# A graph transformer layer on one core: the edge stage's two one-hot matrices, one moved from VectorE to ScalarE, one cut in four

## The chip, the core and the metric

One core of one Trainium2 chip runs the whole program. The metric is the device time of one launch in microseconds (us); lower is better. The engines are TensorE (PE, with its weight loads as PEld), VectorE (DVE), ScalarE (ACT), GpSimd (POOL) and SyncE (SP). Each takes its own instructions in order, and they wait for each other on semaphores.

## What is computed

The reference is a graph neural network of two layers over 6,250 nodes with 128 features and 200,000 edges sorted by destination, with 32 edge types and 16 node types, and 8 heads of 16 features:

```python
def gt_layer(x, ntype, etype, src, dst, ...):
    k = typed_linear(x, ntype, Wk).reshape(n, H, HS)      # q and v alike
    kT = jnp.einsum('nhd,htdo->nhto', k, Watt)            # vT = ... v, Wmsg
    kw = kT[src, :, etype]
    m = vT[src, :, etype]
    a = jnp.einsum('ehd,ehd->eh', kw, q[dst]) * pri[:, etype].T / SQRT_D
    att = edge_softmax(a, dst, n)
    msg = (m * att[:, :, None]).reshape(-1, H * HS)
    hag = jax.ops.segment_sum(msg, dst, num_segments=n)
    h = jax.nn.silu(typed_linear(hag, ntype, Wa))
    alpha = jax.nn.sigmoid(skip[ntype])[:, None]
    h = h * alpha + x * (1.0 - alpha)
    # then mean and variance over the features, scale and shift
```

After two such layers there is a last product, the sum with the input, and a normalisation.

## The kernel before

A first part sorts out the edges (ranks, starts of segments, types). Then a loop over the two layers runs these stages, one after the other: the projections q, k, v; a table with one row for each pair of source node and edge type (`table_d`, 256 numbers to a row, k then v); **the edge stage**; a stage that joins sums across tiles of edges; and the output projection with its normalisation.

The edge stage takes the edges in chunks of 16 tiles (CT) of 128 edges. There are 98 chunks for each of the two layers, 196 in all. Nearly everything in it is double buffered (index b, 0 or 1), and the loop body stands twice, once for each b. A quarter of a chunk is 4 tiles (QT). The order is written out by hand:

- **POOL** issues one indirect DMA for each tile (L903), 16 to a chunk, that gathers the rows of 128 edges out of `table_d` into `kv_e`. It waits for the indices of the chunk (`row_s`, copied by ACT in L999) and, at each quarter, for the values `pv` of the chunk two before (L901), which read the same buffer.
- **SP** loads `local_b` (L915: for each edge of the chunk its rank relative to the tile's first, in bf16, the same 2048 numbers on all 128 partitions) and `q_w` (the q rows of the ranks). It does so two chunks ahead, after the products `qe_ps` of the chunk that used that buffer (L914).
- **PE** multiplies `of_rank` with `q_w` (L1033, one quarter at a time) to spread q from ranks to edges. It does this for chunk c+1 while it is in chunk c: quarters 0 to 2 at the start of its body, and quarter 3 after the transpose of `score` (L1053) and the two products of flags (L1056). Then come the transpose of `prob_t` (L1060) and the sums `sum_ps` (L1067), which multiply `to_rank` with `pv`, 3 tiles to a bank. A product of two f32 tiles is two instructions in the trace.
- **DVE** forms `kq` (L966) and `score` (L969) by quarters as the gathers land, two running maxima (L975, L977), `below` (L980) and the four products `pv` (L985).
- **ACT** copies indices (L999), `score_t` (L1001), takes the exponential (L1003), copies the probabilities into `pv` (L1010), the sums out of PSUM (L1019), and issues the store of the chunk (L1023).

Two matrices of ones and zeros are needed for each chunk, both f32, 128 partitions by 16 tiles by 128. `of_rank` has ranks on the partitions and edges along the row: `local_b` equals the partition's number `part`. DVE makes it in `spread_ranks` (L944), one instruction, for chunk c+2, between `below` and `pv` of chunk c. `to_rank` has edges on the partitions and ranks along the row: `lane` (0 to 127) equals `local_c` of the edge. DVE makes it in `place_edges` (L949), one instruction, for chunk c+1, after quarter 2 of chunk c; it waits for the sums that last read that buffer (`s_used`).

## Time and profile before

| | us |
|---|---|
| median of 3 runs | 8303.22 |
| the runs | 8294.33 to 8305.0 |
| profiled execution: from its first to its last instruction (span) | 7619.3 |
| median less that span | 683.9 |
| edge stage: start of the first to start of the last gather, layer 0 | 1329.92 to 3534.96 |
| the same, layer 1 | 4809.19 to 7010.65 |

The profile gives the execution's time as its span; the program's time on the device holds in addition what lies ahead of the first instruction and behind the last. An engine's busy share is its mean over stages that have different limits, so the edge stage has to be read by itself. In the views each row has the engine, the line of the code, the operation, the tile written and the tiles read, and in brackets the idle time of the engine before the row and what ended it. "Issue" is time in which the engine waited for nothing that the profile shows.

### The profile page before, as it was taken

To read this page: it belongs to the slowest core of one execution; us is meant where nothing else is said; L and a number is where in the kernel's file an instruction comes from. 1 tells how busy PE (TensorE), PEld (TensorE's weight loads), DVE (VectorE), ACT (ScalarE), POOL (GpSimd) and SP (SyncE) were. 2 spreads that over 40 slices of the span, in tenths; PEclk is the share of its full clock that TensorE was granted. 3 is DMA by queue.
4 is the path that set the end of the run, shared out by engine and by line. 5 is a ranking of instruction groups with operands and counts; after the bars stand their busy time and mean duration, and the time that the engine had idled before them with its cause. 6 is when DMAs were issued, how large, how long until landed. Compare 5 with 4: busy or idle time off the path is not lost. (4 is left out here: it accounts for less than half of the span.)

```text
span 7619.3 us, 79126 instructions
## 1 busy us (share of the span) xinstructions
PE 4483.6 (59%) x18423; PEld 3236.2 (42%) x18424; DVE 3763.8 (49%) x5261; ACT 1445.3 (19%) x3714; POOL 4322.7 (57%) x4007
## 2 busy tenths in 40 slices
PE   0128999566666665654318999566666665665221
PEld 0113443555555555554203444455555555555111
DVE  1224443555555555554374444455555555554473
ACT  0013333111111111112112333111111111111111
POOL 0543222777777777775303222677777777776305
PEclk9569999666766666666559999766666666676555
DMA  3125776666666666665103777666666666666101
GB/s 68 39 45 220 297 297 281 160 178 166 177 165 176 167 171 170 170 172 122 29 19 150 297 297 296 181 168 174 169 173 168 176 166 176 169 173 159 34 0 35
DMA packets 809561, 1228.51 MB, mean 161 GB/s; under 512 B 152983, under 2 KB 623978, under 8 KB 758833
## 3 DMA queue, kind: packets, MB, share of 16 engines
q0 software_dynamic: 223248, 853.51, 33.6%
q10 hardware_dynamic: 439680, 221.74, 11.4%
q1 hardware_dynamic: 146097, 148.81, 10.9%
q14 instruction: 528, 4.33, 0.2%
q8 instruction: 8, 0.13, 0.0%
HBM read 574.03 MB, written 649.66 MB: 161 GB/s over the span
## 5 line engine op out<-in xcount | busy, mean ns | idle before, releaser
L903 POOL DMA_INDIRECT kv_e<-table_d,row_s x3136 | 3453.7, 1101 | 982.1 <-issue 939.1
L1033 PE MATMUL qe_ps<-q_w,of_rank 128*128 (+1 forms) x6336 | 1149.3, 340 | 634.5 <-DVE kq L966 565.9
L1067 PE MATMUL sum_ps<-pv,to_rank 128*128 128x136 f32 x6272 | 1193.2, 373 | 261.7 <-DVE pv L985 261.7
L1033 PEld LDWEIGHTS qe_ps<-q_w,of_rank 128*128 128x128 f32 x6336 | 991.3, 240 | 767.4 <-issue 710.9
L966 DVE TENSOR_TENSOR kq<-kv_e,qe_ps 128x512 f32<-128x512 f32 x784 | 537.4, 685 | 1528.8 <-DMA kv_e<-table_d,row_s 1526.7
L1067 PEld LDWEIGHTS sum_ps<-pv,to_rank 128*128 128x128 f32 x6272 | 1154.7, 277 | 318.4 <-issue 318.4
L759 POOL DMA_INDIRECT table_d<-piece,t_row x392 | 372.7, 951 | 1041.9 <-ACT piece L811 829.7
L811 DVE COPY piece<-k_ps 128x512 f32<-128x512 f32 x784 | 541.7, 691 | 808.6 <-PE k_ps L801 808.6
L801 PE MATMUL k_ps<-edge_w,kv_t 128*128 128x512 f32 x1568 | 813.9, 601 | 2.6 <-DVE edge_w L821 2.6
L801 PE MATMUL v_ps<-edge_w,kv_t 128*128 128x512 f32 x1568 | 802.4, 593 | 0.0
L1019 ACT COPY sums<-sum_ps 128x408 f32<-128x408 f32 (+1 forms) x1176 | 522.5, 461 | 943.9 <-PE sum_ps L1067 941.8
L811 ACT COPY piece<-v_ps 128x512 f32<-128x512 f32 x784 | 458.7, 585 | 898.4 <-PE v_ps L801 898.4
L1053 PE MATMUL turn_ps_<-ident,score 128*128 128x128 f32 x196 | 93.0, 475 | 866.9 <-DVE score L969 866.9
L969 DVE TENSOR_REDUCE score<-kq 128x32 f32<-128x512 f32 x784 | 537.8, 686 | 26.9
L985 DVE TENSOR_TENSOR pv<-kv_e,pv 128x512 f32<-128x512 f32 x784 | 491.6, 690 | 24.3 <-ACT pv L1010 0.4
L801 PEld LDWEIGHTS v_ps<-edge_w,kv_t 128*128 128x128 f32 x1568 | 298.4, 190 | 377.0 <-issue 330.2
L951 DVE TENSOR_TENSOR to_rank<-lane,local_c 128x2048 f32<-128x2048 f32 x198 | 452.1, 2283 | 0.0
L801 PEld LDWEIGHTS k_ps<-edge_w,kv_t 128*128 128x128 f32 x1568 | 283.0, 190 | 357.9 <-issue 284.4
L1053 PEld LDWEIGHTS turn_ps_<-ident,score 128*128 128x128 f32 x196 | 35.7, 182 | 912.7 <-DVE score L969 912.7
L999 ACT COPY row_s<-row_c 128x16 int32 x196 | 40.0, 204 | 1751.3 <-DMA kv_e<-table_d,row_s 1751.3
L715 POOL DMA_INDIRECT q_d<-qkv,qrow_i x98 | 95.1, 971 | 407.6 <-DVE qkv L618 407.6
L975 DVE TENSOR_TENSOR_SCAN run_max<-turn_ps_,score_t 128x128 f32<-128x128 f32 x196 | 83.1, 424 | 394.8 <-ACT score_t L1001 394.8
(269 smaller groups left out, 3352.6 us busy)
## 6 DMA issues: line engine op xcount, KB each, us to landing
part_d<-sums ACTq DMA_DIRECT2D x196, 1088.0 KB, 6.4
local_b<-local_d SPq DMA_DIRECT2D x200, 512.0 KB, 6.4
kv_e<-table_d,row_s POOLq DMA_INDIRECT x3136, 2.8
q_w<-q_d SPq DMA_DIRECT2D x200, 64.0 KB
table_d<-piece,t_row POOLq DMA_INDIRECT x392, 4.5
flag<-start_d SPq DMA_DIRECT2D x392, 8.0 KB
q_d<-zero SPq DMA_DIRECT2D x50, 64.0 KB
max_d<-ends_max ACTq DMA_DIRECT2D x196, 1.0 KB, 4.3
```

The lines of the kernel that those rows point to most:

```text
L759: pool.indirect_dma_start(out=piece_rows, out_offset=bass.IndirectOffsetOnAxis(ap=row_s[:, j, q:q + 1], axis=0), in_=piece[:, q].rearrange ...
L801: pe.matmul(bank[:, g % 2, :], kv_t[:, slot[j], a, :], edge_w[:, a, g * TG:(g + 1) * TG, :].rearrange("p t o -> p (t o)"), start=True, sto ...
L811: copy(piece[:, q, o:o + TG, a * D:(a + 1) * D], bank[:, g % 2, :].rearrange("p (t o) -> p t o", t=TG)).then_inc(s_copied, 1)
L903: pool.indirect_dma_start(out=kv_e[:, b, t, :], out_offset=None, in_=table_d, in_offset=bass.IndirectOffsetOnAxis(ap=row_s[:, b, t:t + 1], ...
L951: dve.tensor_tensor(to_rank[:, b], lane[:].unsqueeze(1).broadcast_to([P, CT, P]), local_c[:, ds(c * CT, CT)].unsqueeze(2).broadcast_to([P, ...
L966: dve.tensor_tensor(kq[:, ts], kv_e[:, b, ts, 0:D], qe_ps[:, q * QT * D:(q + 1) * QT * D].rearrange("p (t f) -> p t f", t=QT), ALU.mult).t ...
L969: dve.tensor_reduce(score[:, q * QT * H:(q + 1) * QT * H], kq[:, ts].rearrange("p t (h d) -> p (t h) d", h=H), AX, ALU.add).then_inc(s_sco ...
L985: dve.tensor_tensor(pv[:, b, ts, 0:D].rearrange("p t (h d) -> p t h d", h=H), kv_e[:, b, ts, D:2 * D].rearrange("p t (h d) -> p t h d", h= ...
L1019: last = act.copy(sums[:, b, t0:t1, :], sum_ps[:, n % 3, 0:(t1 - t0) * REC].rearrange("p (t f) -> p t f", f=REC)).then_inc(s_sumc[n % 3], 1)
L1033: last = pe.matmul(qe_ps[:, t * D:(t + 1) * D], of_rank[:, b, t, :], rows, start=True, stop=True)
L1053: pe.transpose(turn_ps[:, 0, :], score[:], ident[:])
L1067: last = pe.matmul(sum_ps[:, n % 3, (t - t0) * REC:(t - t0 + 1) * REC], to_rank[:, b, t, :], pv[:, b, t, :], start=True, stop=True)
```

## The change

`of_rank` is made by ACT, in two passes over 128x2048: the absolute value of (`local_b` minus the partition's number), with a new one-column tile `minus` as bias, and then, in place, the positive part of (1 minus that). The result is 1 where they are equal and 0 elsewhere. The second pass waits for the first on a new semaphore. In the loop both stand at the end of ACT's body, after the store of the chunk; ahead of the loop ACT makes the first two. `to_rank` stays on DVE, in four instructions of 128x512, two after quarter 1 and two after quarter 2.

```diff
-            def spread_ranks(dve, c, b, i):
-                dve.wait_ge(s_loc[b], (i + 1) * 16)
-                dve.tensor_scalar(of_rank[:, b].rearrange("p t e -> p (t e)"), local_b[:, b, :], part[:], None,
-                                  ALU.is_equal).then_inc(s_of[b], 1)
-
-            def place_edges(dve, c, b, i):
+            def spread_ranks(act, b, i):
+                act.wait_ge(s_loc[b], (i + 1) * 16)
+                act.activation(of_rank[:, b].rearrange("p t e -> p (t e)"), local_b[:, b, :], ACT.Abs, bias=minus[:]).then_inc(s_far[b], 1)
+                act.wait_ge(s_far[b], i + 1)
+                act.activation(of_rank[:, b].rearrange("p t e -> p (t e)"), of_rank[:, b].rearrange("p t e -> p (t e)"), ACT.Relu, bias=1.0, scale=-1.0).then_inc(s_of[b], 1)
+
+            def place_edges(dve, c, b, i, q):
                 dve.wait_ge(s_used[b], ONE + i)
-                dve.tensor_tensor(to_rank[:, b], lane[:].unsqueeze(1).broadcast_to([P, CT, P]),
-                                  local_c[:, ds(c * CT, CT)].unsqueeze(2).broadcast_to([P, CT, P]), ALU.is_equal).then_inc(s_to[b], 1)
+                dve.tensor_tensor(to_rank[:, b, q * QT:(q + 1) * QT], lane[:].unsqueeze(1).broadcast_to([P, QT, P]),
+                                  local_c[:, ds(c * CT + q * QT, QT)].unsqueeze(2).broadcast_to([P, QT, P]), ALU.is_equal
+                                  ).then_inc(s_to[b], 1)
...
-                            if q == 2:
-                                place_edges(dve, c + 1, 1 - b, i + b)
+                            if q in (1, 2):
+                                place_edges(dve, c + 1, 1 - b, i + b, 2 * q - 2)
+                                place_edges(dve, c + 1, 1 - b, i + b, 2 * q - 1)
...
-                        spread_ranks(dve, c + 2, b, i + 1)
                         dve.wait_ge(s_pcol[b], i + 1)
...
                         act.dma_start(out_d[ds(c, 1), :, :, :].rearrange("a j t f -> j (a t) f"), sums[:, b]).then_inc(s_out[b], 16)
+                        spread_ranks(act, b, i + 1)
...
-                        pe.wait_ge(s_to[b], i + 1)
+                        pe.wait_ge(s_to[b], (i + 1) * 4)
```

On DVE, in the second half of the loop body (b = 1), from quarter 2 to the products `pv`, the rows of the kernel before are:

```order
L966 TENSOR_TENSOR kq<-kv_e,qe_ps 128x512
L969 TENSOR_REDUCE score<-kq 128x32
L951 ISA
L951 TENSOR_TENSOR to_rank<-lane,local_c 128x2048
L966 TENSOR_TENSOR kq<-kv_e,qe_ps 128x512
L969 TENSOR_REDUCE score<-kq 128x32
L975 SCALAR_TENSOR_TENSOR run_max<-turn_ps_,score_t 128x128
L977 SCALAR_TENSOR_TENSOR rank_max<-turn_ps_,run_max 128x128
L980 TENSOR_TENSOR below<-score_t,rank_max 128x128
L946 TENSOR_SCALAR of_rank<-local_b,part 128x2048
L985 TENSOR_TENSOR pv<-kv_e,pv 128x4x128 x4
```

The same place in the changed kernel, from the end of quarter 1 to quarter 3's product:

```order
L972 TENSOR_REDUCE score<-kq 128x32
L952 REGISTER_ALU
L953 ISA
L953 TENSOR_TENSOR to_rank<-lane,local_c 128x512
L953 ISA
L953 TENSOR_TENSOR to_rank<-lane,local_c 128x512
L969 TENSOR_TENSOR kq<-kv_e,qe_ps 128x512
L972 TENSOR_REDUCE score<-kq 128x32
L953 ISA
L953 TENSOR_TENSOR to_rank<-lane,local_c 128x512
L953 ISA
L953 TENSOR_TENSOR to_rank<-lane,local_c 128x512
```

The long instruction behind quarter 2 has become two pairs of short ones, behind quarters 1 and 2, and nothing stands any more between `below` and `pv`.

On ACT, from the last copies of a chunk's sums (b = 0) to the next chunk's start, the kernel before has, with the semaphores that each row waits for:

```order
L1019 COPY sums<-sum_ps 128x136 [waits e_used0]
L1022 REGISTER_ALU
L1023 ISA [waits e_sumc2,e_sumc1,e_sumc0]
L1023 DMA part_d<-sums 128x16x136
L999 ISA [waits e_kv12,e_kv13,e_kv11,e_kv10]
L999 COPY row_s<-row_c 128x16
```

and the changed kernel:

```order
L1025 COPY sums<-sum_ps 128x136 [waits e_used0]
L1028 REGISTER_ALU
L1029 ISA [waits e_sumc2,e_sumc1,e_sumc0]
L1029 DMA part_d<-sums 128x16x136
L946 REGISTER_ALU
L947 ACTIVATE of_rank<-local_b,minus 128x2048 [waits e_loc0]
L949 ACTIVATE of_rank<-of_rank 128x2048 [waits e_far0]
L1005 ISA [waits e_kv12,e_kv13,e_kv11,e_kv10]
L1005 COPY row_s<-row_c 128x16
```

Two long instructions have come in behind the store and ahead of the wait for the next chunk's gathers.

## Rows read from the trace of the kernel before

**Rows 1.** The page: span, busy us, and busy tenths in 40 slices.
```profile
span 7619.3 us, 79126 instructions
PE 4483.6 (59%) x18423; PEld 3236.2 (42%) x18424; DVE 3763.8 (49%) x5261; ACT 1445.3 (19%) x3714; POOL 4322.7 (57%) x4007
...
POOL 0543222777777777775303222677777777776305
PEclk9569999666766666666559999766666666676555
```

**Rows 2.** Groups of instructions: count, busy us, mean ns of one, idle before.
```profile
L903 POOL DMA_INDIRECT kv_e<-table_d,row_s x3136 | 3453.7, 1101 | 982.1 <-issue 939.1 <-DVE pv L985 43.0
...
L985 DVE TENSOR_TENSOR pv<-kv_e,pv 128x512 f32<-128x512 f32 x784 | 491.6, 690 | 24.3 <-ACT pv L1010 0.4
...
L951 DVE TENSOR_TENSOR to_rank<-lane,local_c 128x2048 f32<-128x2048 f32 x198 | 452.1, 2283 | 0.0
...
L946 DVE TENSOR_SCALAR of_rank<-local_b,part 128x2048 f32<-128x2048 bf16 x200 | 257.5, 1287 | 38.3 <-DMA local_b<-local_d 38.3
```

**Rows 3.** The tile kv_e: shortest, median and longest gather, first and last start.
```profile
L903 POOL DMA_INDIRECT kv_e<-table_d,row_s x3136: 942/946/3054, 1329.9 to 7010.7; - x196
```

**Rows 4.** Timeline at one to_rank: start, us, engine, line [idle before].
```profile
2406.80 2.28 DVE L951 TENSOR_TENSOR to_rank<-lane,local_c 128x2048 f32<-128x2048 f32 x1
2407.49 2.40 POOL L903 DMA_INDIRECT kv_e<-table_d,row_s  x1 [0.30 <-issue]
```

**Rows 5.** Timeline, the same chunk, from the transpose of score to the store.
```profile
2413.31 0.47 PE L1053 MATMUL turn_ps_<-ident,score 128*128 128x128 f32 x1 [5.84 <-DVE score L969]
...
2414.86 2.08 PE L1033 MATMUL qe_ps<-q_w,of_rank 128*128 x8
...
2416.39 1.32 DVE L946 TENSOR_SCALAR of_rank<-local_b,part 128x2048 f32<-128x2048 bf16 x1
2416.45 1.38 POOL L903 DMA_INDIRECT kv_e<-table_d,row_s  x1 [0.30 <-issue]
...
2417.79 2.54 DVE L985 TENSOR_TENSOR pv<-kv_e,pv 128x512 f32<-128x512 f32 x4
2418.13 1.17 POOL L903 DMA_INDIRECT kv_e<-table_d,row_s  x1 [0.31 <-issue]
...
2418.73 5.69 PE L1067 MATMUL sum_ps<-pv,to_rank 128*128 128x136 f32 x32 [1.38 <-DVE pv L985]
2419.61 0.95 POOL L903 DMA_INDIRECT kv_e<-table_d,row_s  x1 [0.30 <-issue]
...
2420.48 0.50 ACT L1019 COPY sums<-sum_ps 128x408 f32<-128x408 f32 x1 [2.73 <-PE sum_ps L1067]
...
2421.84 0.50 ACT L1019 COPY sums<-sum_ps 128x408 f32<-128x408 f32 x1 [0.86 <-PE sum_ps L1067]
...
2425.13 0.39 ACTq L1023 DMA_DIRECT2D part_d<-sums  x1
```

**Rows 6.** Timeline, 22 us earlier: quarters 0 to 2 of the next chunk's product.
```profile
2403.26 2.02 PE L1033 MATMUL qe_ps<-q_w,of_rank 128*128 128x128 f32 x16
...
2406.31 1.15 PE L1033 MATMUL qe_ps<-q_w,of_rank 128*128 x8 [1.03 <-DVE kq L966]
```

**Rows 7.** The chunk after: its gather in to_rank, and its wait for indices.
```profile
2430.99 2.28 DVE L951 TENSOR_TENSOR to_rank<-lane,local_c 128x2048 f32<-128x2048 f32 x1
2432.09 1.99 POOL L903 DMA_INDIRECT kv_e<-table_d,row_s  x1 [0.30 <-issue]
...
2434.05 0.20 ACT L999 COPY row_s<-row_c 128x16 int32 x1 [9.15 <-DMA kv_e<-table_d,row_s]
```

**Rows 8.** Groups of ACT's instructions, SBUF to SBUF, in other stages.
```profile
L628 ACT ACTIVATE hag<-h_sb 128x3200 f32<-128x3200 f32 x2 | 5.7, 2872 | 150.8 <-DVE h_sb L647 150.8
...
L1138 ACT ACTIVATE tile_lm<-tile_lm 128x1568 f32<-128x1568 f32 x2 | 3.0, 1510 | 10.8 <-DVE tile_lm L1161 10.8
```

**Rows 9.** DMA issues: KB each, median us to landing.
```profile
part_d<-sums ACTq DMA_DIRECT2D x196, 1088.0 KB, 6.4
```

More of the change, by code:

```diff
@@ L857, in program @@
         to_rank = sb(st, "to_rank", [P, 2, CT, P])
+        minus = sb(st, "minus", [P, 1])
         kq = sb(st, "kq", [P, CT, D])
@@ L875, in program @@
             (s_idx, s_q, s_loc, s_flag, s_of, s_to, s_qe, s_kq, s_score, s_turn, s_turned, s_scan, s_below, s_exp,
-             s_prob, s_pcol, s_used, s_ends, s_endsd, s_out, s_go) = (two(n) for n in (
+             s_prob, s_pcol, s_used, s_ends, s_endsd, s_out, s_go, s_far) = (two(n) for n in (
                  "idx", "q", "loc", "flag", "of", "to", "qe", "kq", "score", "turn", "turned", "scan", "below",
-                 "exp", "prob", "pcol", "used", "ends", "endsd", "out", "go"))
-            s_win = sem("e_win")
+                 "exp", "prob", "pcol", "used", "ends", "endsd", "out", "go", "far"))
+            s_win, s_minus = sem("e_win"), sem("e_minus")
             s_kv = [[sem(f"e_kv{b}{q}") for q in range(4)] for b in range(2)]
@@ L942, in _ @@
                     sp.wait_ge(s_q[b], (NCH // 2 + 1) * 16)
-            def spread_ranks(dve, c, b, i):
-                dve.wait_ge(s_loc[b], (i + 1) * 16)
-                dve.tensor_scalar(of_rank[:, b].rearrange("p t e -> p (t e)"), local_b[:, b, :], part[:], None,
-                                  ALU.is_equal).then_inc(s_of[b], 1)
-            def place_edges(dve, c, b, i):
+            def spread_ranks(act, b, i):
[4 more added lines that the diff above has]
+            def place_edges(dve, c, b, i, q):
                 dve.wait_ge(s_used[b], ONE + i)
-                dve.tensor_tensor(to_rank[:, b], lane[:].unsqueeze(1).broadcast_to([P, CT, P]),
-                                  local_c[:, ds(c * CT, CT)].unsqueeze(2).broadcast_to([P, CT, P]), ALU.is_equal).then_inc(s_to[b], 1)
+                dve.tensor_tensor(to_rank[:, b, q * QT:(q + 1) * QT], lane[:].unsqueeze(1).broadcast_to([P, QT, P]),
+                                  local_c[:, ds(c * CT + q * QT, QT)].unsqueeze(2).broadcast_to([P, QT, P]), ALU.is_equal
+                                  ).then_inc(s_to[b], 1)
             @block.vector
             def _(dve):
-                for b in range(2):
-                    spread_ranks(dve, b, b, 0)
-                place_edges(dve, 0, 0, 0)
+                dve.tensor_scalar(minus[:], part[:], -1.0, None, ALU.mult).then_inc(s_minus, 1)
+                for q in range(4):
+                    place_edges(dve, 0, 0, 0, q)
                 with dve.Fori(0, NCH // 2) as i:
@@ L993, in _ @@
                     act.copy(row_s[:, b, :], row_c[:, b * CT:(b + 1) * CT]).then_inc(s_idx[b], 1)
+                act.wait_ge(s_minus, 1)
+                for b in range(2):
+                    spread_ranks(act, b, 0)
                 with act.Fori(0, NCH // 2) as i:
```

## The prediction

> **What bounds the kernel now.** I read the stage's length first. The two stretches of gathers last 2205 and 2201 us of the span of 7619.3, and nothing outside them is edited, so only they count. The page's means do not tell what limits them (POOL 57%, PE 59%, DVE 49%) [rows 1]. The group of gathers does: 3136 of them, 1101 ns each, with 982.1 us of idle time between them, 0.31 each, nearly all "issue" [rows 2]. A chunk is 16 x (1.101 + 0.313) = 22.6 us with the two entries into the stage, 22.5 by the stretches (4406.5 / 196 = 22.48). POOL thus never waits for data inside the stage; in the timeline every gather starts 0.30 or 0.31 us after the last one ended. **POOL's issue of gathers sets the time**, and a microsecond taken from it in each chunk is worth 196 us.
>
> Next I look at what makes a gather long. The median is 946 ns, the longest 3054 [rows 3], the mean 1101 [rows 2]: 3136 x 0.155 = 486 us lie above the median, 2.5 us a chunk. The timeline shows where. A gather that starts 0.69 us into the instruction that writes `to_rank` takes 2.40 us and ends 0.80 us after it, as if only its first 0.15 us had been done before [rows 4]; the one a chunk later takes 1.99 and also ends 0.81 after [rows 7]. A gather that starts with `of_rank` takes 1.38, and the next, which starts 0.34 us into the four `pv` products, 1.17; the one after that starts 1.82 us into them, and takes the undisturbed 0.95 [rows 5]. Sorted in this way, the timeline's 3136 gathers (first and last in [rows 3]) give: 196 held by `to_rank`, 295 us together, **1.5 us a chunk**; 198 held by `of_rank`, 157 us, **0.8 a chunk**; the rest 38 us, mostly `pv`, **0.2 a chunk**. Without stalls a chunk would be 16 x (0.946 + 0.305) = **20.0 us**.
>
> The Trainium skill ("SBUF — State Buffer", section Who interferes with whom) has the rule for this: a VectorE instruction with two SBUF inputs contends with a GpSimd instruction that reads SBUF, one in a two-port mode with any, and the shared port is held for the whole instruction. The trace agrees for both kinds [rows 4, 5].
>
> **The change, part by part.**
>
> *`of_rank` leaves DVE.* That takes 1.29 us of DVE work from between `below` and `pv` of each chunk [rows 2], and the stall with it: the sorting above leaves nothing of the 486 us for ACT, which copies 0.50 us at a time beside the gathers [rows 5]. Gain 0.8 us a chunk. `pv` itself waits for the copy of probabilities and does not start earlier, so nothing on PE's side gains.
>
> *`to_rank` in four.* A DVE instruction of 128x512 with such operands takes 0.69 (`pv`, [rows 2]), so four are 2.76 in place of 2.28. DVE then has 0.8 us a chunk less work than before in all, and is idle about half of the time [rows 1]: it costs nothing. What counts is how long a gather is held. It is caught at one point early in its life, and then for the rest of the short instruction. Bounds for a chunk: zero, if no gather's start falls into the pieces; above, each pair lasts 1.4 us, about one gather period, so it catches one or two gathers for at most 0.45 us each, 1.8 for both pairs. The nearest row is `pv`, four such pieces back to back, which cost the gather 0.22 and the following one nothing [rows 5]: so the port is let go between the pieces. I take 0.2 for each pair, 0.4 together, instead of 1.5. `pv` was partly shielded, since `of_rank` had just set POOL's phase; I raise it from 0.2 to 0.3, bounds 0.2 and 0.6. Sum of stalls: 0.4 + 0.3 = **0.7 us a chunk** (from 0.3 to 2.2) in place of 2.5.
>
> *ACT's two passes.* ACT takes 1510 ns for 128x1568 and 2872 for 128x3200 [rows 8], 0.835 ns an element, so 1.91 us for 2048; two with a semaphore between them, 3.9 us. Reading bf16 is not in the trace; I take the same. ACT stands idle for 9.15 us ahead of the next index copy [rows 7], so the copy of indices is not late. No table load comes with them in ACT's order. Here is a rule that speaks against the change: the Trainium skill ("ScalarE: Activation LUTs", section Rules for kernel authors) wants relu on VectorE, where it is up to three times faster. The trace agrees on the price (1.29 against 3.9 us), but by [rows 2] DVE's instruction also stops POOL. The same page (What ACT_TABLE_LOAD costs) gives about 1990 ns for such a pass with a bias by pointer, which would add 0.2 us to the ring below.
>
> *The new wait.* PE's quarters 0 to 2 for the next chunk need the new `of_rank`, which ACT now makes behind the store. Before, they followed the sums at once. Now: the sums end at 2424.42, the store is issued at 2425.13 and takes 0.39 [rows 5], then 3.9 us: PE starts about **5.1 us after the sums**. Behind its wait stand quarters 0 to 2, then L1053 and all of the chunk's chain. The cover is PE's idle time before L1053, 5.84 us [rows 5]. This closes a ring: L1053 to the end of the sums 11.1 us [rows 5] + 5.1 + quarters 0 to 2. These were 2.02 + 1.15 = 3.2 us [rows 6] at the high clock; at the low one a quarter is 2.08 [rows 5], so 6.2. The ring is 19.4 to 22.4 us. As long as it is under POOL's 20.7, nothing shows; above, it becomes the period. The granted clock in the stage reads 0.6 to 0.7 [rows 1], between the levels 0.5 (1.2 GHz) and 1 (2.4 GHz). In the row of sums the first two copies are 1.36 us apart; at that pace 16 tiles would take 7.25, and they took 5.69 [rows 5]: the clock rose under way, after 3 to 4 us of dense work. If quarters 0 to 2 do the same, they take 3.7 + 0.41 x 3.2 = 5.0, and the sums, now behind denser work, about 1 us less (wholly at the high clock 3.7). That is 11.1 + 5.1 + 5.0 - 1.0 = **20.2 us**: under POOL's period, by little.
>
> *Ends of the stage.* The first `of_rank` is 2.6 us later, but the first `kq` waits for gathers anyway; the last two passes lie under the landing of the store, 6.4 us [rows 9]. Both zero.
>
> **Sum.** 20.0 + 0.7 = 20.7 us a chunk against 22.5: 1.8 x 196 = 353 us. The span goes from 7619.3 to about 7266; with the 683.9 outside it, as in the median of the runs, the time from 8303 to **7950**.
>
> **The rivals.**
>
> 1. *The ring sets the period (PE waits for ACT, ACT for PE).* For it: 20.2 is an estimate between 19.4 and 22.4, and POOL can wait for `pv` of two chunks before (L901). Against it: when PE is late it has no idle time before L1053, and dense work raised the clock in the row of sums. With the ring at 21.0 to 22.3 the time is 8010 to 8265, centre 8090.
> 2. *Short pieces still stall POOL.* If the port is not let go between two pieces, each pair holds a gather for up to 1.2, with `pv` 2.2 in all: period 22.2, time 8245; if half of that, 8100. Against: the 0.95 gather within `pv` [rows 5].
> 3. *Slower.* The gap of 5 us leaves PE at the low clock throughout: quarters 6.2, sums 7.25. The ring is then 11.1 + 1.6 + 5.1 + 6.2 = 24.0, 1.5 over the old period: 8303 + 290 = 8600. It decides from a ring of 22.5, that is when sums and quarters together lose more than 1.3 us against [rows 5] and my 5.0 us. Against: the sums would have to be slower than before though more work stands ahead of them.
> 4. *Nothing changes*, since ring or another wait comes out at 22.4 to 22.6: for it only the ring's upper bound.
>
> **How the numbers follow.** Forecast 0.60 (7870 to 8040), rival 1 0.24, rival 2 0.08, slower 0.05, no change 0.03. The range of 8 in 10 is 7870 to 8160: it holds the forecast's own bounds of stalls (0.3 to 1.1 us) and the lower half of rivals 1 and 2. A difference of 0.2% (17 us) is about what a measurement of this kernel can tell from no change. Faster by more than that: 0.60 + 0.24 + 0.08 = 0.92, less 0.01 for the top of rival 1: 0.91. Same 0.04, slower 0.05.
>
> **What would show it.** Right: the mean of a gather falls from 1101 to about 990 ns; its idle time stays at 0.31 and "issue"; no gather over about 1.6 us in the stage; DVE's `to_rank` about 690 ns each; ACT's passes about 1.9 us; PE's idle time before L1060 (the old L1053) a few tenths, put down to `score`. Rival 1: gathers as short, but POOL waits for `pv`, and PE's row before the transpose of `score` has no idle time. Rival 2: gathers of 1.5 to 2 us beside the pairs. Rival 3: PE's clock at 0.5 all through the stage. The forecast is wrong if ACT's pass over bf16 takes well over 2 us, or if the time of a chunk is over 21.2.

## The result: 3.9% slower in the comparison, 5.0% faster on another chip

| kernel | us, median | range |
|---|---|---|
| before | 8298.77 | 8278.49 to 8305.0 |
| changed | 8613.93 | 8610.93 to 8617.45 |

The changed kernel takes 1.0386 of the time before, with a 95% interval of 1.0346 to 1.0425. The prediction was 7950 and faster; it was wrong.

One fact has to stand ahead of all numbers. The experiments below fell on six chips, and these show two kinds. On chips 13 and 6 the kernel before takes 7627 to 7631 us (medians of the jobs), on chips 10, 9, 4 and 7 it takes 8278 to 8319, and no execution of it lay between 7638 and 8227. Only chip 10 was met in two jobs, so whether it is the chip or something else of the job that makes the kind is not shown. So every time below stands beside the kernel before of its own job. The kernel before, on record at 8303 us, and its profile with a span of 7619.3 [rows 1] are one of each kind. I call the kinds **prompt** (7630) and **late** (8300), for the reason shown below; the texts of expectation say "first chip" and "second chip".

The page of the changed kernel's profiled execution, of the late kind (span, busy us, and busy tenths in 40 slices, as in [rows 1]):

```profile
span 8609.1 us, 80616 instructions
PE 4410.2 (51%) x18423; PEld 3276.0 (38%) x18424; DVE 3533.9 (41%) x5657; ACT 2219.3 (26%) x4114; POOL 3955.2 (46%) x4007
...
POOL 0632224555555555554203223555555555555304
PEclk9579997777677767776559998776766666766655
```

This execution took 8610.93 us, 1.8 more than its span. So only some 2 us lie outside the span, not the 683.9 that the prediction put there.

Groups of instructions of the same execution (busy us, mean ns | idle before and what ended it), beside [rows 2]:

```profile
L904 POOL DMA_INDIRECT kv_e<-table_d,row_s x3136 | 3085.6, 984 | 2272.8 <-DVE pv L988 1329.3 <-issue 929.5 <-ACT row_s L1005 14.0
...
L953 DVE TENSOR_TENSOR to_rank<-lane,local_c 128x512 f32<-128x512 f32 x792 | 511.9, 688 | 452.9 <-PE sum_ps L1074 319.8 <-remote 71.2 <-issue 61.9
...
L988 DVE TENSOR_TENSOR pv<-kv_e,pv 128x512 f32<-128x512 f32 x784 | 489.5, 687 | 261.0 <-ACT pv L1016 261.0
```

A gather has become short, as forecast: 984 ns instead of 1101. But POOL, whose gaps in [rows 2] are 0.31 us each, now waits for `pv` 1329.3 us. The longest waits of DVE, ACT and POOL (us in total, times, longest us):

```profile
DVE run_max L979 <- ACT score_t L1007: 2351.0, 196, 13.8
ACT score_t L1007 <- remote: 2305.8, 192, 13.6
POOL kv_e L904 <- DVE pv L988: 1329.3, 192, 10.3
```

"Remote" is not an engine. ACT's copy of `score_t` waits for nothing but the semaphore of the transposes on PE; the word says that when it was released no instruction had just ended. The timeline of one chunk shows it (start, us, engine, line [idle before]):

```profile
2419.29 0.27 PE L1060 MATMUL turn_ps_<-ident,score 128*128 128x128 f32 x1
2419.50 0.71 PE L1063 MATMUL turn_ps_<-flag,spread 16*128 16x128 f32 x4
...
2423.64 0.95 POOL L904 DMA_INDIRECT kv_e<-table_d,row_s  x1 [0.30 <-issue]
2427.27 0.27 ACT L1007 COPY score_t<-turn_ps_ 128x128 f32<-128x128 f32 x1 [12.33 <-remote]
...
2430.11 2.50 DVE L988 TENSOR_TENSOR pv<-kv_e,pv 128x512 f32<-128x512 f32 x4 [1.34 <-ACT pv L1016]
2430.94 6.03 PE L1074 MATMUL sum_ps<-pv,to_rank 128*128 128x136 f32 x32 [1.29 <-DVE pv L988]
2431.59 1.24 POOL L904 DMA_INDIRECT kv_e<-table_d,row_s  x1 [7.01 <-DVE pv L988]
...
2443.47 5.46 PE L1040 MATMUL qe_ps<-q_w,of_rank 128*128 128x128 f32 x24 [6.50 <-ACT of_rank L949]
...
2448.72 0.33 PE L1060 MATMUL turn_ps_<-ident,score 128*128 128x128 f32 x1
```

PE is done with the flags at 2420.21, and ACT starts at 2427.27, 7.06 us later. In between POOL issues its last gathers; the last begins at 2423.64, and then POOL is stuck behind `pv`. The trace also records when each semaphore rises. The one of the flags' products rises at 2427.25, in one burst with three others of PE, of which the oldest had been due since 2418.56. The ends of PE's instructions are modelled in the trace, so one has to ask whether the products themselves came late. The burst speaks against it: by their rows the four products end over 2.7 us (2418.56 to 2421.29), and their semaphores rise within 0.25. Over all chunks the lateness has a median of 5.65 us (4.7 to 7.5 in nine of ten), and it is found only where PE raises the semaphore. Where ACT or DVE raise it, the next engine starts at once: `run_max` 0.03 us after the copy of `score_t`, and the exponential 0.03 after `below`, in all 196 chunks.

In every one of the 192 late chunks ACT's copy starts 2.2 to 3.0 us after the end of the last gather, and in nine of ten 0.8 to 1.5 after the end of the last packet of POOL's DMA queue. So in this kernel the semaphores come when the stream of gathers has run out; the trace does not tell whether POOL's issuing or the traffic of its gathers counts.

### The profile page after: what moved, and what is told of

It is laid out like the page before. It is cut to its first block and busy times, and to the rows that moved or that the text cites. A ratio compares the mean times of both kernels' runs of the same rounds, so it can differ in the third digit from the quotient of the medians.

```text
span 8609.1 us, 80616 instructions
## 1 busy us (share of the span) xinstructions
PE 4410.2 (51%) x18423; PEld 3276.0 (38%) x18424; DVE 3533.9 (41%) x5657; ACT 2219.3 (26%) x4114; POOL 3955.2 (46%) x4007
## 5 line engine op out<-in xcount | busy, mean ns | idle before, releaser
L904 POOL DMA_INDIRECT kv_e<-table_d,row_s x3136 | 3085.6, 984 | 2272.8 <-DVE pv L988 1329.3
L1040 PE MATMUL qe_ps<-q_w,of_rank 128*128 (+1 forms) x6336 | 1256.8, 380 | 1206.1 <-ACT of_rank L949 1128.9
L1040 PEld LDWEIGHTS qe_ps<-q_w,of_rank 128*128 128x128 f32 x6336 | 1172.7, 286 | 1268.0 <-issue 702.0
L1074 PE MATMUL sum_ps<-pv,to_rank 128*128 128x136 f32 x6272 | 1135.0, 360 | 263.3 <-DVE pv L988 263.3
L1074 PEld LDWEIGHTS sum_ps<-pv,to_rank 128*128 128x128 f32 x6272 | 1096.5, 265 | 319.8 <-issue 319.8
L1067 PE MATMUL turn_ps_<-ident,prob_t 128*128 128x128 f32 x196 | 92.9, 474 | 1287.6 <-ACT prob_t L1009 1287.6
L953 DVE TENSOR_TENSOR to_rank<-lane,local_c 128x512 f32<-128x512 f32 x792 | 511.9, 688 | 452.9 <-PE sum_ps L1074 319.8
L1007 ACT COPY score_t<-turn_ps_ 128x128 f32<-128x128 f32 x196 | 52.2, 266 | 2364.2 <-remote 2305.8
L1067 PEld LDWEIGHTS turn_ps_<-ident,prob_t 128*128 128x128 f32 x196 | 35.6, 182 | 1324.9 <-ACT prob_t L1009 1324.9
L947 ACT ACTIVATE of_rank<-local_b,minus 128x2048 f32<-128x2048 bf16 x200 | 400.4, 2002 | 145.5 <-ACT sums L1025 84.3
```

The costliest lines, as they stand in the source:

```text
L904: pool.indirect_dma_start(out=kv_e[:, b, t, :], out_offset=None, in_=table_d, in_offset=bass.IndirectOffsetOnAxis(ap=row_s[:, b, t:t + 1], ...
L947: act.activation(of_rank[:, b].rearrange("p t e -> p (t e)"), local_b[:, b, :], ACT.Abs, bias=minus[:]).then_inc(s_far[b], 1)
L953: dve.tensor_tensor(to_rank[:, b, q * QT:(q + 1) * QT], lane[:].unsqueeze(1).broadcast_to([P, QT, P]), local_c[:, ds(c * CT + q * QT, QT)] ...
L1040: last = pe.matmul(qe_ps[:, t * D:(t + 1) * D], of_rank[:, b, t, :], rows, start=True, stop=True)
L1074: last = pe.matmul(sum_ps[:, n % 3, (t - t0) * REC:(t - t0 + 1) * REC], to_rank[:, b, t, :], pv[:, b, t, :], start=True, stop=True)
```

## Experiments

Letters stand for theories. A is the ring through ACT (PE waits for `of_rank`, rivals 1 and 3 of the prediction). B is that the pairs of short instructions hold up POOL. D came up after the first late runs: an unbroken stream of gathers on POOL holds back PE's semaphores.

The diffs show the lines that matter; new tiles, new semaphores and their start values are left out.

### The kernel before, and each half of the change by itself (chip 13, prompt)

e1 is the kernel before once more. e2 has only `to_rank` in four:

```diff
-                            if q == 2:
-                                place_edges(dve, c + 1, 1 - b, i + b)
+                            if q in (1, 2):
+                                place_edges(dve, c + 1, 1 - b, i + b, 2 * q - 2)
+                                place_edges(dve, c + 1, 1 - b, i + b, 2 * q - 1)
```

e3 has only `of_rank` on ACT:

```diff
-                        spread_ranks(dve, c + 2, b, i + 1)
...
+                        spread_ranks(act, b, i + 1)
```

e4 is e2 with two passes of the same size and form added to ACT at that place, on tiles that nobody reads, while DVE still makes `of_rank`:

```diff
+                        act.activation(idle_rank[:], lane_w[:], ACT.Abs, bias=part[:]).then_inc(s_idle, 1)
+                        act.wait_ge(s_idle, c * 2 + 1)
+                        act.activation(idle_rank[:], idle_rank[:], ACT.Relu, bias=1.0, scale=-1.0).then_inc(s_idle, 1)
+                        act.wait_ge(s_idle, c * 2 + 2)
```

> The kernel before, profiled a second time. Its profile had a span of 7619 us beside runs of 8299, and the changed kernel's span is 8609 beside 8614. If 684 us lie outside the span of this program, the span is again about 7619 and the time about 8300. If the first profile caught an execution that differs from the timed ones, the span is now about 8297, and the gathers have idle time that ends on pv, or the copy of score_t waits several us more than the 2.8 us of the first profile.

> Only the cut of to_rank into four, of_rank stays on DVE. Theory A (the new wait of PE for ACT makes the ring the period): no ring is closed here, so the time is under the kernel before. If POOL's issue sets the time of the timed runs too, a chunk loses 1.1 us of stalls: 8300 - 215 = about 8085. Theory B (the pairs of short instructions on DVE are what is late): slower than before, towards 8600. Theory C (the timed runs of before are not set by POOL's stalls): within 0.5% of before.

> Only the move of of_rank to ACT, to_rank stays one instruction on DVE. Theory A: the whole loss is here, 8550 to 8650, a chunk at about 27 us, and POOL waits for pv of two chunks before. Theory B: about the time of before or under it.

> of_rank stays on DVE and to_rank is cut in four; ACT makes two passes of 128x2048 at the same place behind the store, but over a constant into a tile that nobody reads, so that PE does not wait for them (extra work, nothing left out). Theory A (it is PE's wait): the same time as with the cut alone. Rival (ACT is too busy, its other copies come late): about 8600.

| run | us | ratio to before (7631.13) | 95% |
|---|---|---|---|
| e1 before | 7631.45 | 1.0001 | 0.9991 to 1.0011 |
| e2 split only | 7376.36 | 0.9668 | 0.9652 to 0.9684 |
| e3 ACT only | 7473.41 | 0.9798 | 0.9781 to 0.9814 |
| e4 split, ACT busy beside it | 7375.62 | 0.9668 | 0.9652 to 0.9684 |

This was the surprise that opened the case: the kernel that had been timed at 8299 ran at 7631, and the pieces of a change that had cost 3.9% were both gains. Groups of e2:

```profile
L903 POOL DMA_INDIRECT kv_e<-table_d,row_s x3136 | 3216.5, 1026 | 982.1 <-issue 959.9 <-DVE pv L988 22.3
```

and of e3:

```profile
L904 POOL DMA_INDIRECT kv_e<-table_d,row_s x3136 | 3311.5, 1056 | 982.2 <-issue 962.4 <-DVE pv L985 19.8
...
L947 ACT ACTIVATE of_rank<-local_b,minus 128x2048 f32<-128x2048 bf16 x200 | 400.3, 2002 | 146.0 <-ACT sums L1022 139.1 <-DMA local_b<-local_d 6.9
L949 ACT ACTIVATE of_rank<-of_rank 128x2048 f32<-128x2048 f32 x200 | 381.9, 1910 | 6.3
```

In both, POOL's idle time is the 982 us of [rows 2], 0.31 for each gather, and only the gathers' busy time falls. The split gives 254.8 us, 1.30 a chunk; ACT gives 157.7, 0.80 a chunk. e4 shows that two passes of ACT, when nobody waits for them, cost nothing beside the gathers (0.7 us of 7376). A and B have no room here: POOL has no wait beyond its usual gaps, and what the pairs still hold up is within the mean of 1026.

### The same on a late chip (chip 10)

> The changed kernel a second time. In the last experiments the kernel before took 7631 us, as in its first profile, and not 8299 as in the comparison of the change; there each half of the change alone gained 2 and 3.3%. If the changed kernel's loss belongs to the executions in which the kernel before takes 8299, it now takes the forecast's share: both halves together remove the stalls, 20.7 us a chunk, 7631 - 353 = about 7280, with score_t copied about 2 us after its transpose. If the ring of PE and ACT is slow by itself when both halves are there, it is again about 8610, with a copy of score_t 12 us after PE's first quarter.

> The cut of to_rank alone, beside the changed kernel in the same job. If the kernel before is again at 7631: about 7376, and above the changed kernel by about 100. If the kernel before is at 8299 in this job: this shows whether the slower executions take the gain of the cut away (then within 1% of 8299).

> The kernel before, profiled in the same job as the two kernels below, so that all three are read on one chip. The jobs so far fell on two chips: on one the kernel before takes 7631 us and TensorE's semaphores are raised 0.01 us after its products end; on the other it takes 8308, and in the changed kernel the products of quarters 1 to 3 and the flags end 6 to 10 us before their semaphores rise. If this job is on the second chip: a period of about 25.9 us a chunk, with such late semaphores too, but fewer. If it is on the first: 7631.

> The changed kernel. On the first chip: POOL's gathers set the period, stalls of 0.6 to 0.7 us a chunk, 20.7 us a chunk, about 7280 (the theory that the late semaphores make the whole loss); a ring of PE and ACT above that gives 7340 to 7600. On the second chip: again 8615.

| run | us | before in the job | ratio | 95% |
|---|---|---|---|---|
| e5 changed kernel | 8618.23 | 8307.55 | 1.0380 | 1.0353 to 1.0408 |
| e6 split only | 8579.48 | 8307.55 | 1.0335 | 1.0299 to 1.0370 |
| e7 before | 8316.39 | 8301.51 | 1.0015 | 0.9989 to 1.0041 |
| e8 changed kernel | 8619.03 | 8301.51 | 1.0402 | 1.0366 to 1.0439 |

The same text of e2 that gained 3.3% loses 3.3% here. The group of gathers in e6:

```profile
L903 POOL DMA_INDIRECT kv_e<-table_d,row_s x3136 | 3069.1, 979 | 2261.8 <-DVE pv L988 1316.1 <-issue 943.5 <-ACT row_s L1002 2.1
```

e6 has no work on ACT at all, so the loss is not the ring through ACT as I had drawn it. What it shares with the changed kernel is the wait for `pv`, and 2863.5 us in which ACT's copy of `score_t` is released by "remote". The kernel before has the same illness, in part of its chunks. Its gathers in e7:

```profile
L903 POOL DMA_INDIRECT kv_e<-table_d,row_s x3136 | 3349.3, 1068 | 1703.2 <-issue 973.0 <-DVE pv L985 730.1
```

and its timeline, one bad chunk (from 2417) and the start of the next:

```profile
2417.52 1.22 PE L1056 MATMUL turn_ps_<-flag,spread 16*128 16x128 f32 x4
...
2429.70 0.27 ACT L1001 COPY score_t<-turn_ps_ 128x128 f32<-128x128 f32 x1 [14.50 <-remote]
...
2434.02 1.24 POOL L903 DMA_INDIRECT kv_e<-table_d,row_s  x1 [7.46 <-DVE pv L985]
```

The flags end at 2418.74 and are seen at 2429.70, 11 us late. POOL waits for `pv` in 74 chunks of 196 here, and in 192 in the changed kernel. Not all of these late copies of `score_t` wait for the end of the stream: of the 64 that start over 1 us late, a quarter start within 0.25 us of a gather's end.

### Does breaking the stream release the semaphores? (chip 10)

e9 is the changed kernel with one unused fill on POOL ahead of gather 12 of each chunk:

```diff
+                            if t == 12:
+                                pool.memset(pause[:], 0.0).then_inc(s_pause, 1)
+                                pool.wait_ge(s_pause, i * 2 + b + 1)
```

> The changed kernel, with GpSimd writing zeros to an unused tile of 128x2048 before the last four gathers of each chunk, about 2 us in which it issues none (extra work, nothing left out). Theory D (on the second chip TensorE's semaphores rise only once the stream of gathers breaks off): they rise in the pause, the copy of score_t comes some 5 us earlier, and in spite of the pause the time is 200 to 900 us under the 8615 of the changed kernel. Rival (the delay is of a fixed length, or due to the density of TensorE's instructions): the time stays at 8615 or rises by up to 400. On the first chip the pause is only added: 196 x 2 = 400 us above the changed kernel.

8445.57 us (two runs, 8417.38 and 8473.76), 1.0193 of before (1.0127 to 1.0260), 173 less than e8 in the same job, a little under the 200 to 900 that I expected. Its groups:

```profile
L908 POOL DMA_INDIRECT kv_e<-table_d,row_s x3136 | 3059.8, 976 | 1758.4 <-issue 1011.9 <-DVE pv L992 693.9 <-POOL pause L902 52.0
...
L902 POOL MEMSET pause<- 128x2048 f32 x196 | 357.1, 1822 | 0.1
```

357 us of useless work were put on the engine that was thought to bound the kernel, and it became faster. POOL's wait for `pv` fell from 1326 (e8) to 694 us, in 95 chunks instead of 192. So the pattern of POOL's instructions, or of the traffic that its gathers start, has a part in when PE's semaphores are seen. No theory of the prediction has that.

### The changed kernel on a prompt chip (chip 6)

> The changed kernel, in a new job. On the chip where the kernel before takes 7631: 7260 to 7340, POOL's gathers back to back at 20.7 us a chunk, score_t copied within 3 us after its transpose starts. On the chip where it takes 8300: 8618 again.

> Only the move of of_rank to ACT; to_rank stays one instruction of 2.3 us that holds a gather for 1.5 us in each chunk. On the first chip 7473 again. On the second, theory D (an unbroken stream of gathers keeps TensorE's semaphores back, and each hold of the stream lets them through): under the cut alone (8579) and the changed kernel (8618), near the 8300 of the kernel before, since the long hold is still there. Rival (the ring over ACT makes the loss there): 8550 or more, as the changed kernel.

e12 paces the stream with a fill of 128x512 before each quarter:

```diff
+                            if t % QT == 0:
+                                pool.memset(pause[:], 0.0).then_inc(s_pause, 1)
+                                pool.wait_ge(s_pause, i * 8 + b * 4 + t // QT + 1)
```

> The changed kernel, with GpSimd writing zeros to an unused tile of 128x512 before each quarter's gathers, four pauses of about 0.6 us in a chunk where the pause of 1.8 us stood once (extra work, nothing left out). On the first chip POOL's period is longer by four such writes: 196 x 2.6 = 500 us over the changed kernel. On the second, theory D in the form that any break in the stream helps: as with the one pause, 8350 to 8500. If only a long break drains what is held back: 8600 or more.

| run | us | ratio to before (7627.31) | 95% |
|---|---|---|---|
| e10 changed kernel | 7246.10 | 0.9499 | 0.9472 to 0.9527 |
| e11 ACT only | 7470.11 | 0.9793 | 0.9764 to 0.9821 |
| e12 changed, paced | 8110.86 | 1.0633 | 1.0602 to 1.0664 |

Here the forecast stands: its span was about 7266, and the measured one is 7246.7 (for e10 I had expected 7260 to 7340). The page of e10:

```profile
span 7246.7 us, 80616 instructions
PE 4294.4 (59%) x18423; PEld 3176.4 (44%) x18424; DVE 3564.0 (49%) x5657; ACT 2229.5 (31%) x4114; POOL 3950.5 (55%) x4007
...
PEclk9559999777777777776558999877777777776555
```

its gathers, as a group:

```profile
L904 POOL DMA_INDIRECT kv_e<-table_d,row_s x3136 | 3082.2, 983 | 982.4 <-issue 961.7 <-DVE pv L988 20.7
```

as a tile (shortest, median, longest), against 942/946/3054 in [rows 3]:

```profile
L904 POOL DMA_INDIRECT kv_e<-table_d,row_s x3136: 942/946/1468, 1330.8 to 6639.0; - x196
```

and once round the ring in its timeline:

```profile
2406.21 0.27 PE L1060 MATMUL turn_ps_<-ident,score 128*128 128x128 f32 x1
2406.41 0.71 PE L1063 MATMUL turn_ps_<-flag,spread 16*128 16x128 f32 x4
...
2407.16 0.27 ACT L1007 COPY score_t<-turn_ps_ 128x128 f32<-128x128 f32 x1 [2.27 <-PE turn_ps_ L1063]
...
2410.95 5.63 PE L1074 MATMUL sum_ps<-pv,to_rank 128*128 128x136 f32 x32 [1.53 <-DVE pv L988]
...
2421.91 4.71 PE L1040 MATMUL qe_ps<-q_w,of_rank 128*128 128x128 f32 x24 [5.33 <-ACT of_rank L949]
...
2426.47 0.33 PE L1060 MATMUL turn_ps_<-ident,score 128*128 128x128 f32 x1
```

Gathers 983 ns, gaps 0.31, none over 1.47 us; the flags end at 2407.12 and are seen at 2407.16, as in all 196 chunks of every prompt run. The ring in this round, from one L1060 to the next, is 20.26 us, and POOL's chunk (3082.2 + 982.4) / 196 = 20.74. The two are nearly tied: PE's wait for `score` before L1060, 5.84 us in [rows 5], is down to 116.6 us in all, 0.6 a chunk.

e12 tells what time on POOL is worth when POOL does bound the kernel:

```profile
L908 POOL DMA_INDIRECT kv_e<-table_d,row_s x3136 | 3083.1, 983 | 1398.9 <-issue 762.2 <-POOL pause L902 636.7
...
L902 POOL MEMSET pause<- 128x512 f32 x784 | 425.0, 542 | 26.1 <-issue 25.8
```

The gathers are unchanged and POOL's busy and idle time grew by 425.0 + 26.1 + (1398.9 - 982.4) = 868 us; the time grew by 865. The 500 expected left out that after each fill POOL waits 0.81 us (636.7 / 784) instead of 0.30. Fills cost all their time here, and a fill gave time back on chip 10. The two kinds have different bounds.

### A wait instead of a fill, and half the data (chip 9, late)

e14 lets POOL go on to gather 12 only when the chunk before has had its `score` transposed. e15 gathers 128 numbers instead of 256 for each edge, out of other rows, and `pv` is made from what was gathered instead of from the v half, so its values are not the reference's.

```diff
+                            if t == 12:
+                                pool.wait_ge(s_turned[1 - b], ONE + i + b)
```

```diff
-                            pool.indirect_dma_start(out=kv_e[:, b, t, :], out_offset=None, in_=table_d,
+                            pool.indirect_dma_start(out=kv_e[:, b, t, 0:D], out_offset=None, in_=table_d.rearrange("r (a f) -> (r a) f", a=2),
```

> Only the move of of_rank to ACT, wanted on the second chip (the one where the kernel before takes 8300). Theory D (an unbroken stream of gathers keeps back TensorE's semaphores; the long to_rank instruction breaks it): 8250 to 8500, under the 8579 of the cut alone and the 8618 of both. Rival (on this chip the ring over ACT costs as much by itself): 8550 or more. On the first chip 7470 again, which tells nothing new.

> The changed kernel; POOL in addition waits, before the last four gathers of a chunk, until ACT has copied score_t of the chunk before. On the first chip that copy is made long before, by the fourth gather: no change, 7246. On the second, theory D: the stream breaks off after 12 gathers in place of 16, TensorE's semaphores rise some 2.5 us later, and the last four gathers are issued beside scans and pv, where POOL stood idle for 7 us: 3 us a chunk less, 7900 to 8300. Rival (the delay has nothing to do with the stream): later still than 8618, as POOL stands twice.

> The changed kernel with gathers of half the row, 128 numbers of 256 (the products pv take the same half twice; the values are left out and other rows are read). POOL issues as many gathers in the same time, but the DMA engines move half the bytes. On the first chip POOL's issue still sets the time: 7200 to 7250. On the second: if the bytes that the gathers move keep TensorE's semaphores back, the loss goes and the time is 7250 to 7500; if it is POOL's issue or the number of rows and semaphore writes, which stay, 8550 to 8620.

| run | us | ratio to before (8277.51) | 95% |
|---|---|---|---|
| e13 ACT only | 8610.05 | 1.0409 | 1.0340 to 1.0478 |
| e14 changed, waits at gather 12 | 8295.13 | 1.0027 | 0.9995 to 1.0059 |
| e15 changed, half the numbers | 8653.26 | 1.0462 | 1.0399 to 1.0524 |

e13 refutes a part of D: I had thought that the long `to_rank`, which holds a gather for up to 2 us, breaks the stream and so protects the kernel before. e13 has the long `to_rank` and is as slow as the changed kernel. Its semaphores are late in another way. The flags are over 1 us late in only 93 chunks (median over all 0.84), half of those are seen within 0.2 us of a gather's end, in the midst of the stream, and the copy of `prob_t`'s transpose into `pv` (L1013) comes late too: 1.40 us after the product in the median, against 0.29 in e10. Its gathers:

```profile
L904 POOL DMA_INDIRECT kv_e<-table_d,row_s x3136 | 3306.7, 1054 | 2027.1 <-DVE pv L985 1068.7 <-issue 957.5 <-ACT row_s L1002 0.9
```

e15 says that it is not the bytes: with half of them the wait for `pv` is no shorter, 1404.8 us. e14 is some 320 us under the changed kernel's 8614 to 8619 on other late chips, and its timeline shows why:

```profile
2414.88 0.71 PE L1065 MATMUL turn_ps_<-flag,spread 16*128 16x128 f32 x4
...
2415.62 0.27 ACT L1009 COPY score_t<-turn_ps_ 128x128 f32<-128x128 f32 x1 [6.42 <-PE turn_ps_ L1065]
...
2416.70 0.95 POOL L906 DMA_INDIRECT kv_e<-table_d,row_s  x1 [5.79 <-ACT score_t L1009]
```

While POOL stands still, the flags' semaphore is seen 0.03 us after the products (2415.59 to 2415.62). Over all chunks ACT starts 0.04 us after them in the median and 0.99 at most, in 155 of 196 within 0.05: the row put down to "remote" for 2305.8 us is gone. But lateness has moved to the other semaphores of PE: DVE's `to_rank` now waits 1206.8 us for "remote".

### The wait in the kernel before, and the last two runs (chips 4 and 7, late)

e16 puts the same wait into the kernel before; e17 and e18 are e14 again.

> The kernel before with one wait of POOL ahead of a chunk's gather 12, for the copy score_t of the chunk before; nothing else is changed. Two kinds of chip have been seen. On the kind where TensorE's semaphores rise late (before about 8300): if the unbroken stream of gathers holds them back, the wait breaks the stream at a set place, score_t is copied within 0.1 us of the flags' products, and the time goes below before's own by 100 us or more (about 8000 to 8200). If the lateness has nothing to do with the stream, the wait only takes time from POOL: 8300 to 8500. On the kind where they rise in time (before about 7630): POOL at gather 12 is 16 to 17 us into a chunk of 22.5 and the score of the chunk before is turned at about 6 to 8 us, so the wait is always met: 7631, within 0.3%.

> The changed kernel with the same wait, as run before in e14. On the kind of chip with late semaphores: 8295 again, equal to the kernel before. On the other kind: gather 12 of a chunk starts about 15.5 us after the chunk's first gather and score_t of the chunk before is there by 8 us at the latest, so the wait costs nothing and the time is that of the changed kernel there, 7246, within 0.3%. If it costs on that kind what the paced kernel lost (865), it comes out near 8100, and the waits of POOL themselves are what hurts there.

> The same kernel as e14 and e17: the changed kernel with POOL's wait for score_t ahead of gather 12. Seen twice, both times beside a kernel before of about 8300: 8295 and 8312. If before runs at about 7630 here, the wait should always be met (gather 12 starts about 15.5 us after a chunk's first gather, score_t is there by 8 us) and the time is 7246, within 0.3%; about 8100, the loss of the paced kernel, if waits of POOL themselves cost on that kind of chip. If before runs at about 8300 here, 8300 again.

| run | chip | us | before in the job | ratio | 95% |
|---|---|---|---|---|---|
| e16 before, waits at gather 12 | 4 | 8189.75 | 8291.93 | 0.9897 | 0.9826 to 0.9968 |
| e17 changed, the same | 4 | 8311.79 | 8291.93 | 1.0018 | 0.9991 to 1.0046 |
| e18 changed, the same | 7 | 8020.51 | 8319.25 | 0.9656 | 0.9594 to 0.9718 |

The gathers of e16:

```profile
L905 POOL DMA_INDIRECT kv_e<-table_d,row_s x3136 | 3421.0, 1091 | 1546.7 <-issue 965.0 <-ACT score_t L1003 557.1 <-DVE pv L987 24.7
```

and of e18:

```profile
L906 POOL DMA_INDIRECT kv_e<-table_d,row_s x3136 | 3106.1, 990 | 1682.2 <-issue 880.9 <-ACT score_t L1009 758.9 <-DVE pv L990 42.3
```

A wait that does nothing but stop POOL makes the kernel before 1.0% faster: a small gain, but all four runs (8181 to 8242) lie below the fastest of the 13 of before (8253). D has it so, though half of its `score_t` copies (97) still follow "remote". The changed kernel with it is equal to before in e14 and e17, and 3.4% faster than before in e18. All three fell on late chips, so what the wait costs on a prompt one is not known.

### One sum for all runs

POOL's time for a chunk is its own work (busy time of the gathers and fills, their ordinary gaps) plus its waits for `pv` or `score_t`, each from the group of gathers, divided by 196 (on prompt chips the few gaps put down to `pv` are of ordinary length and count as such):

| run | own work | waits | sum |
|---|---|---|---|
| e1 before, prompt | 22.7 | 0 | 22.7 |
| e2 split, prompt | 21.4 | 0 | 21.4 |
| e3 ACT, prompt | 21.9 | 0 | 21.9 |
| e10 changed, prompt | 20.7 | 0 | 20.7 |
| e7 before, late | 22.1 | 3.7 | 25.8 |
| changed, late | 20.6 | 6.8 | 27.3 |
| e6 split, late | 20.5 | 6.7 | 27.2 |
| e13 ACT, late | 21.8 | 5.5 | 27.2 |
| e15 half the numbers, late | 20.4 | 7.2 | 27.5 |
| e9 pause, late | 22.9 | 3.5 | 26.4 |
| e14 wait, late | 20.2 | 5.5 | 25.7 |
| e17 wait, late | 20.2 | 5.7 | 25.9 |
| e16 before and wait, late | 22.4 | 3.0 | 25.3 |
| e18 wait, late | 20.3 | 4.1 | 24.4 |

The sums give the times: 196 x (27.3 - 25.8) = 294 us more for the changed kernel against e7, measured 8613.93 - 8298.77 = 315. Own work fell by 1.5 us a chunk, close to the forecast's 1.8, and the waits rose by 3.1. On late chips each chunk of the changed kernel ends the same way: 16 gathers in a row, 20.6 us; only then do the flags' semaphores come; then scan, exponential and `pv`, 6.8 us in which POOL stands. The work that was saved in POOL was time in which the chain could not advance anyway. That tells why it gained nothing; why the late semaphores strike in 192 chunks after the change and in 74 before it, and nearly as often with either half alone (191 in e6, 165 in e13), is not explained.

## Why the prediction was wrong, point by point

**The step that failed: "with the 683.9 outside it, as in the median of the runs".** The prediction had a span of 7619.3 and a time of 8303, and put the difference outside the span without a row for it. Where span and time are of one execution they agree: 8609.1 and 8610.93 above, 7246.7 and 7248.53 in e10, 7634.2 and 7635.98 in e1, 1.8 us apart each time. Nearly all of the 684 us lay inside the stage, 3.1 us a chunk (25.8 against 22.7 in the table above), which is waits that this profile did not contain: in it the flags are seen 0.04 us after their end in all 196 chunks. The argument was right for the execution it was read from, and the number was asked for another.

**What bounds the kernel.** "POOL thus never waits for data inside the stage" holds on prompt chips, and only there. On late ones the kernel before waits 730.1 us for `pv` (e7), and the microseconds taken from POOL's own work there (1.5 a chunk) came back as waits, with 1.6 more.

**Stalls.** Forecast: `to_rank` 1.5 down to 0.4, `of_rank` 0.8 down to 0, 0.7 left. Measured on prompt chips: 1.30 for the split (1.1 was forecast), 0.80 for ACT, and 16 x (0.983 - 0.946) = 0.6 left. The sum of both halves alone is 412 us, both together gave 381 (7627.3 to 7246.1); the forecast was 353. The gathers are as short on late chips (984 ns), so this part held everywhere. The rule of the Trainium skill ("SBUF — State Buffer", section Who interferes with whom), by which the port is held for the whole of one instruction, agrees with both halves: with `to_rank` in four the longest gather is 2013 ns (e2), and with `of_rank` gone from DVE too it is 1468 (e10), against 3054.

**ACT's passes.** Forecast 1.91 each; measured 2.00 with the bias tile over bf16 and 1.91 in place. The Trainium skill ("ScalarE: Activation LUTs", What ACT_TABLE_LOAD costs) gives about 1990 ns for the first, and the trace agrees with 2002. The two together are the 3.9 us of the forecast; only the first has its bias by pointer, so the 0.2 us that the prediction held ready for both was 0.1.

**The ring.** Forecast 20.2 us, under POOL's 20.7 "by little". In e10's round it is 20.26: 4.74 from L1060 to the sums, 5.63 of sums, 5.33 of gap (5.1 forecast), 4.56 from quarter 0 to the next L1060 (5.0 forecast). That the total agrees so well is in part luck: the 1.0 taken off for faster sums did not come there (5.63 against 5.69 in [rows 5]), and the way to the sums was 0.7 shorter instead (4.74 against 5.42). On the late chip the round shown above is 29.4 us: 11.65, 6.03, 6.50 and 5.25 to the next L1060. So on late chips the term of the ring that was mis-sized is "L1053 to the end of the sums": with 7 us between the flags and their copy it is 17.7 instead of the 10.1 that I took (11.1 less 1.0).

**The rivals.** Rival 3 gave 8600, and 8614 came, but not by its mechanism: it has PE at the clock's lower level, 0.5, all through the stage, and there the granted clock is 0.70 to 0.71, above the 0.68 of the profile before; the sums took 6.03 us, not 7.25. That agreement is chance. Rival 1's sign (POOL waits for `pv`) is there, at a price that it did not hold, since it took the chain from the flags to `pv` as fixed. And e6, without ACT's passes, has the same wait.

## What to carry to other kernels

Set the span beside the timed runs before anything else. If they differ by more than a few microseconds, the profile shows another execution than the one to be predicted; price the gap as unknown waits inside the loop and widen the range by it, on both sides. Here this would have left "POOL bounds" as one of two cases.

Work saved on an engine that runs far ahead is a gain only if what it waits for is ready sooner. When the same edit gives opposite signs in two jobs, look at the time of the kernel before in each job first. And where a consumer is released by nothing ("remote"), compare the end of the producer with the consumer's start before blaming either.

## What the runs showed of the hardware

- The same kernel took 7627 to 7631 us on two chips and 8278 to 8319 on four. In the traces the kinds differ in when PE's semaphores rise: median lateness for the flags 0.01 us in e10, 5.65 in the changed kernel on a late chip, 0.60 with POOL's wait in e18. Engines that waited for ACT or DVE started as promptly on both kinds.
- They differ in one thing more. The traces of the eight prompt executions (the first profile among them) hold 102,590 to 104,445 records of semaphores rising, those of the twelve late ones 35,797 to 49,474, with the same number of DMA packets (809,573 to 809,575; fewer in e15 alone). Records are missing ahead of the edge stage as well: 8,433 in the changed kernel's first 1344 us, against 11,348 in the first 1331 of e10. A semaphore's rise is therefore read here together with the start of the engine that waits for it. All executions come with a span, so no run tells whether the recording has a part in the lateness.
- The lateness depends on what POOL does (e9, e14 and e16 against e8 and e7), not on how many bytes its gathers move (e15, where the stage moves some 101 GB/s instead of 139). Whenever POOL stops, the traffic of its gathers ends soon after, and e15 has as many gathers as before; so POOL's issuing and the transfers that follow from it were never told apart. How long it lasts is not explained: e14 and e18 are the same kernel, 8295 and 8021 us.
- **Left open:** what holds the semaphores back, why on some chips, and why each half of the change makes it worse. That the stream of gathers is the cause is supported by three kernels in which stopping POOL helped, one of them the kernel before, but not shown. D's form in which a long stall lets the semaphores through fell with e13, and the copies of `score_t` that start amid the stream (e7, e13) do not fit a stream that must first end. No run took the gathers off POOL altogether, which would be the direct test, and the version with the wait was not seen on a prompt chip.
